# An adaLN block with attention and experts on one core: softmax inverses spread by DMA, copies and splits moved between engines

## The reference

```python
h = layernorm(x) * (1 + ca) + sa                    # x: 8 x 512 x 128
q, k, v = h @ Wq.T, h @ Wk.T, h @ Wv.T              # 16 heads of 64
q, k = l2norm(q) * q_scale, l2norm(k) * k_scale
attn = softmax(q @ k.T * 64 ** -0.5)                # 16 x 512 x 512 in each batch
x = x + ga * ((attn @ v) @ Wo.T + bo)
h = layernorm(x) * (1 + cb) + sb
x = x + gb * (moe(h))                               # top 2 of 8 experts with capacities, plus a shared expert
```

## Time and profile before

| | |
|---|---|
| median of 3 runs | 1409.95 us (1408.2 to 1410.84) |
| profiled execution | 1406.78 us, of which the span of the core is 1405.0 us |
| busy share of the span | TensorE 90%, VectorE 79%, ScalarE 68%, GpSimd 61% |
| mean granted TensorE clock | 0.959 of full speed |

### The profile page before, as it was taken

How to read it: one execution, slowest core, us unless ns; L and a number is a source line. 1 busy time by engine, 2 the same in 40 slices (tenths; PEclk the granted TensorE clock), 3 DMA queues, 4 the chain that set the end, 5 groups by cost and what they waited for, 6 DMA issues and landing times. The chain is left out here.

```text
span 1405.0 us, 31811 instructions
## 1 busy us (share of the span) xinstructions
PE 1262.1 (90%) x9674; PEld 828.6 (59%) x9674; DVE 1107.3 (79%) x1995; ACT 952.9 (68%) x2014; POOL 858.0 (61%) x1659
## 2 busy tenths in 40 slices
PE   4899999989999999999899999999994477899997
PEld 4555565656555565556566555666552355677775
DVE  3778878878878887788788788877873996788887
ACT  3677677767666776677677766777762565777776
POOL 2577666766666776666667667676754664444443
PEclk8899999999999999999999999999998699999999
DMA  5000000000000000000000000000002000535341
GB/s 131 2 2 1 2 1 2 2 4 2 1 4 2 2 2 4 2 2 2 4 1 2 3 2 2 2 1 2 2 1 75 1 0 9 131 86 104 89 89 38
DMA packets 53202, 28.60 MB, mean 20 GB/s; under 512 B 8720, under 2 KB 51224, under 8 KB 53016
## 3 DMA queue, kind: packets, MB, share of 16 engines
q1 hardware_dynamic: 51832, 25.99, 7.7%
q10 hardware_dynamic: 1184, 0.40, 0.1%
HBM read 24.16 MB, written 2.23 MB: 19 GB/s over the span
## 5 line engine op out<-in xcount | busy, mean ns | idle before, releaser
L697 ACT ACTIVATE probs<-bank,neg_max 128x512 f32<-128x512 f32 x512 | 347.5, 684 | 280.3 <-DVE neg_max L815 259.5
L815 DVE TENSOR_REDUCE neg_max<-bank 128x1 f32<-128x512 f32 x512 | 329.3, 685 | 165.4 <-PE bank L516 162.0
L556 PE MATMUL bank<-probsT,qkv 128*64 128x512 f32 x1024 | 280.7, 628 | 0.9 <-DVE oT L832 0.9
L516 PE MATMUL bank<-operands 64*128 64x512 f32 x1536 | 255.9, 439 | 0.9 <-DVE operands L810 0.5
L993 POOL TENSOR_TENSOR inv_wide<-inv_sum,consts 128x512 f32<-128x512 f32 x64 | 66.5, 1039 | 237.7 <-DVE inv_sum L826 237.7
L532 PEld LDWEIGHTS T<-ident,probs 64*128 64x128 f32 x4096 | 173.6, 142 | 40.3 <-issue 10.2
L532 PE MATMUL T<-ident,probs 64*128 64x64 f32 x4096 | 173.6, 226 | 1.5 <-issue 0.7
L486 PEld LDWEIGHTS bank<-operands,hT_h 128*128 128x128 f32 x254 | 48.2, 190 | 213.0 <-issue 209.4
L516 PEld LDWEIGHTS bank<-operands 64*128 64x128 f32 x1536 | 128.4, 190 | 63.5 <-issue 44.2
L1627 POOL TENSOR_TENSOR hid_l<-gated,hid_h 128x512 fp32r<-128x512 f32 x64 | 89.4, 1397 | 123.3 <-ACT hid_h L1544 123.3
L977 POOL TENSOR_TENSOR sq<-qkv 128x256 f32<-128x256 f32 x252 | 150.9, 615 | 11.9 <-ACT qkv L676 9.7
(11 more groups left out here) (235 smaller groups left out, 2399.7 us busy)
## 6 DMA issues: line engine op xcount, KB each, us to landing
probsT<-gate_scratch SPq DMA_DIRECT2D x64, 256.0 KB, 4.9
out<-x_all SPq DMA_DIRECT2D x8, 256.0 KB, 2.3
probsT<-in_L_ffn_fc_w SPq DMA_DIRECT2D x1, 1024.0 KB, 9.4
raw<-in_L_attn_Wq SPq DMA_DIRECT2D x1, 512.0 KB, 4.4
raw<-in_L_attn_Wk SPq DMA_DIRECT2D x1, 512.0 KB, 7.3
raw<-in_L_attn_Wv SPq DMA_DIRECT2D x1, 512.0 KB, 8.6
raw_o<-in_L_attn_Wo SPq DMA_DIRECT2D x1, 512.0 KB, 8.7
probsT<-in_L_ffn_sh_w SPq DMA_DIRECT2D x2, 256.0 KB, 2.7
```

Of the source, the lines that this page charges most:

```text
L516: last = nc.tensor.matmul(s_bank(hp, 2 * pair + head)[:], own[rows, q, toks], own[rows, k], start=((q, k) == (QH, KH)), stop=(q == QL))
L556: last = nc.tensor.matmul(O_BANK[rows, :], qkv[:, hp % 4, j, cols], probsT[:, hp % 2, head, j], start=(j == 0), stop=(j == NT - 1), skip_g ...
L697: nc.scalar.activation(probs[:, i % 4], s_bank(hp, i)[:], ACT.Exp, bias=neg_max[:, i:i + 1], accum_out=row_sum[:, hp % 2, i:i + 1]).then_i ...
L815: nc.vector.reduce_max(neg_max[:, i:i + 1], s_bank(hp, i)[:], AX.X, negate=True).then_inc(max_done, 1)
```

## The change

Four things. VectorE's copy of pair 2 goes to ScalarE, so ScalarE copies pairs 1, 2 and 3 and VectorE pair 0; ScalarE does pair 2 in pair 0 of the next slot, behind that pair's two exponentials, and no longer copies inverses. The inverses don't go through GpSimd, TensorE and ScalarE: SyncE writes the 128 x 8 inverses of a unit to DRAM, waits until they are there, and reads them back with two DMAs, one for each head, each spread over 64 partitions; VectorE's `normalise` waits for both. `ln_rows` is written with `scalar_tensor_tensor`, whose second operand is the inverse deviation broadcast over the row, in place of `tensor_scalar` with two scalars per partition. And `split_h1` moves from VectorE to GpSimd, at the end of head pair 5, all four tiles in a row; the high part is a multiplication by one.

```diff
                 for t in range(NT):
-                    last = nc.vector.tensor_scalar(h_ln[:, t], tile_of(b, t), mean_var[:, t, 0:1], rstd[:, t:t + 1],
-                                                   ALU.subtract, ALU.mult)
+                    last = nc.vector.scalar_tensor_tensor(out=h_ln[:, t], in0=tile_of(b, t), scalar=mean_var[:, t, 0:1],
+                                                          in1=rstd[:, t:t + 1].to_broadcast([P, C]), op0=ALU.subtract,
+                                                          op1=ALU.mult)
...
                 def _(sp):
+                    def spread_inverse(w, hp):
+
+                        sp.wait_ge(inv_done, w + 1)
+                        sp.dma_start(inv_scratch[hp % 2].rearrange("k q -> q k"), inv_sum[:, hp % 2]).then_inc(inv_out, 16)
+                        sp.wait_ge(inv_out, 16 * (w + 1))
+                        for head in range(2):
+                            sp.dma_start(inv_row[head * DH:(head + 1) * DH, hp % 2].rearrange("p (t q) -> p t q", t=NT),
+                                         inv_scratch[hp % 2].rearrange("(t h) q -> h t q", h=2)[head].partition_broadcast(DH)
+                                         ).then_inc(inv_in, 16)
...
                     def transpose_probs(u, pair):
-                        before, count = ((t_act, 0), (t_dve, 1), (t_act, 1), (t_dve, 2))[pair]
-                        after(pe, before, 2 * u + count)
+                        before, value = ((t_act, 3 * u), (t_dve, u + 1), (t_act, 3 * u + 1), (t_act, 3 * u + 2))[pair]
+                        after(pe, before, value)
...
-                            if pair == 1 and earlier >= 1:
-                                inverse_rows(u - 1, side)
-                                side = (r_copied, u)
...
-                            if pair == 1 and earlier >= 1:
-                                copy_inverse(u - 1, hp - 1)
...
-                            if pair == 1 and earlier >= 1:
-                                copy_transposed(u - 1, hp - 1, 3)
+                            if pair < 2 and earlier >= 1:
+                                copy_transposed(u - 1, hp - 1, pair + 2)
...
                     def normalise(u, hp):
                         dve.wait_ge(av_step, NT * (u + 1))
-                        dve.wait_ge(r_copied, u + 1)
+                        dve.wait_ge(inv_in, 32 * (u + 1))
...
-                            if pair == 0 and earlier >= 1:
-                                copy_transposed(u - 1, hp - 1, 2)
...
-                        if earlier >= 1:
-                            widen(u - 1, hp - 1)
...
+                        nc.gpsimd.tensor_tensor(hT_h[:, toks], h1_out[:, toks], c1.to_broadcast([P, P]), ALU.mult).then_inc(h1h_done, 1)
+                        pool.wait_ge(h1h_done, NT * b + t + 1)
+                        nc.gpsimd.tensor_tensor(hT_l[:, toks], h1_out[:, toks], hT_h[:, toks].bitcast(F32),
+                                                ALU.subtract).then_inc(hT_ready, 1)
...
+                        if main and hp == HP - 3 and not is_const(b, LAST):
+                            for t in range(NT):
+                                split_h1(b + 1, t)
```

More of the change, by code:

```diff
@@ L400, in adaln_attention_moe @@
             inv_done = sem("inv_done")
-            wide_done = sem("wide_done")
-            r_ready = sem("r_ready")
-            r_copied = sem("r_copied")
+            inv_out = sem("inv_out")
+            inv_in = sem("inv_in")
             av_step = sem("av_step")
@@ L467, in _, with batch @@
                 def _(sp):
+                    def spread_inverse(w, hp):
[6 more added lines that the diff above has]
+                                         ).then_inc(inv_in, 16)
+                    def batch(b):
+                        for hp in range(HP):
+                            if not (is_const(b, 0) and hp == 0):
+                                spread_inverse(HP * b + hp - 1, hp - 1)
+                    over_batches(sp, batch)
+                    spread_inverse(HP * B - 1, HP - 1)
                     sp.wait_ge(av_step, NT * HP * B)
@@ L535, in transpose_probs @@
                         last.then_inc(t_ready, 1)
[L537 to L545, removed]
                     def weigh_values(u, hp, j):
                         if j == 0:
-                            pe.wait_ge(t_dve, 2 * (u + 1))
-                            pe.wait_ge(t_act, 2 * (u + 1))
+                            pe.wait_ge(t_dve, u + 1)
+                            pe.wait_ge(t_act, 3 * (u + 1))
                             after(pe, o_done, u)
@@ L824, in invert_sums @@
                         dve.wait_ge(p_done, S_TILES * (u + 1))
-                        after(dve, wide_done, u - 1)
+                        after(dve, inv_out, 16 * (u - 1))
                         nc.vector.reciprocal(inv_sum[:, hp % 2], row_sum[:, hp % 2]).then_inc(inv_done, 1)
@@ L838, in take_mod @@
                         last.then_inc(done, 1)
[L840 to L844, removed]
-                        dve.wait_ge(h1h_done, NT * b + t + 1)
-                        nc.vector.tensor_tensor(hT_l[:, toks], h1_out[:, toks], hT_h[:, toks].bitcast(F32),
-                                                ALU.subtract).then_inc(hT_ready, 1)
                     def add_y(b, k):
@@ L897, in norm_first @@
                             ln_rows(dve, *rows)
-                        if not is_const(b, LAST) and (hp, pair) in ((5, 1), (5, 2), (5, 3), (6, 0)):
-                            split_h1(b + 1, (pair - 1) % NT)
                     def norm_last(b, hp, pair):
@@ L927, in slot @@
                                 row_max(u, hp, 2 * pair)
+                                if pair == 0 and hp == YT_HP and not is_const(b, 0):
+                                    dve.wait_ge(x1_done, b)
                                 row_max(u, hp, 2 * pair + 1)
@@ L932, in slot @@
                                 low_k(u + 1, hp + 1)
-                            if main and pair == 0 and hp == YT_HP and not is_const(b, 0):
-                                dve.wait_ge(x1_done, b)
-                            if pair == 0 and earlier >= 1:
-                                copy_transposed(u - 1, hp - 1, 2)
                             if pair == 2 and main:
@@ L946, in _ @@
                     take_mod(mod1, (CA, SA), 0, mod1_done, (h1_done, 0))
-                    for t in range(NT):
-                        split_h1(0, t)
                     sum_squares(0)
@@ L987, in normalise_qk, with split_h1 @@
                             nc.gpsimd.tensor_tensor(rows, rows, by, ALU.mult).then_inc(qn_done, 1)
-                    def widen(u, hp):
-                        pool.wait_ge(inv_done, u + 1)
-                        after(pool, r_ready, u)
-                        src = inv_sum[:, hp % 2].rearrange("p (t h) -> p t h", h=2)
-                        nc.gpsimd.tensor_tensor(inv_wide[:], src.unsqueeze(3).to_broadcast([P, NT, 2, DH]),
-                                                c1.unsqueeze(2).unsqueeze(3).to_broadcast([P, NT, 2, DH]),
-                                                ALU.mult).then_inc(wide_done, 1)
+                    def split_h1(b, t):
+                        pool.wait_ge(h1_done, b + 1)
+                        after(pool, pj_ready, NT * (HP * b - 1) + t + 1)
+                        toks = slice(t * P, (t + 1) * P)
+                        nc.gpsimd.tensor_tensor(hT_h[:, toks], h1_out[:, toks], c1.to_broadcast([P, P]), ALU.mult).then_inc(h1h_done, 1)
+                        pool.wait_ge(h1h_done, NT * b + t + 1)
+                        nc.gpsimd.tensor_tensor(hT_l[:, toks], h1_out[:, toks], hT_h[:, toks].bitcast(F32),
+                                                ALU.subtract).then_inc(hT_ready, 1)
                     def split_o(u, hp):
@@ L1025, in batch @@
                             slot(b, hp)
+                    for t in range(NT):
+                        split_h1(0, t)
                     normalise_qk(0, 0)
```

8 lines of the change are left out of this document (2 added, 6 removed).

## The result

The changed kernel takes 1447.7 us (1445.2 to 1450.4), the one before on the same chip 1410.4. The ratio is 1.026, with a 95% interval of 1.023 to 1.029: slower by 37 us, where 15 us less were predicted, and outside the range.

A forecast was written before the change was run, and what follows sets the result against it. TensorE, busy for 90% of the span, was taken as nearly full. With the transposes' gain eaten by the copy's wait, 9 us net and 6 us from earlier scaled Q made 15 us less: 1395 us, range 1371 to 1415.

The forecast's parts named there:

- the DMAs: Per unit, one 4 KB write and two reads: chain some 10 us, needed some 20 us later, so no cost.
- the inverses: Transposes gone from TensorE in pair 1: 34 us if nothing replaced them; GpSimd's earlier scaled Q: 6 us.
- the copy: In pair 1, TensorE's transposes wait for ScalarE's copy of pair 2: 4.68 us a batch against 4.24 removed.
- VectorE's relief: VectorE loses a 1.22 us copy per slot, mostly hidden; earlier layer-norm rows win 0.5 and 0.4 us in head pairs 0 and 3.
- The rival that counted on the clock to stay up: Behind shorter layer-norm stands in head pairs 1 and 4, 15 places win 1.6 us each: 24 us more, 1371; chance 0.25.
- Rows and splits: Layer-norm rows stay 3.07 us; splits on GpSimd cost nothing, and 0.3 us is felt ahead of head pair 6's maxima.
- ScalarE as the bound: Rival: pair 1 rests on ScalarE's exponentials and copy; 0.5 us more per slot gives 1427; chance 0.18.
- The inverses come late: Rival: a DMA chain of over 20 us makes normalising wait in every slot; at 25 us, over 1500; chance 0.02.
- four signs named as wrong: Pair 1 3.0 us everywhere; clock up behind layer-norm rows; normalising waiting for a DMA; the copy's wait pushing pair 2.

The follow-up runs named there:

- run 8: Not a follow-up run: in "make the run 8 bytes or longer" it means a stretch of contiguous bytes in a DMA write, 8 bytes long.

## Why the prediction was wrong

**The step that failed is the DMAs.** The prediction sized the write by a load of 4 KB that landed after 4.7 us, looked only at who waits for the data, found 20 us of slack and wrote "Hidden, so nothing". The write took 9.6 us, and its chain with the reads (3.5 us) is inside the bounds of 5 to 15. In the loop the data was indeed in time. But the write has a second price that the step didn't ask for: what it does to engines that don't wait for it. While it is under way some of TensorE's semaphore updates come up to 3.7 us late, and ScalarE and VectorE stand for them. Of the 47.5 us between the profiled spans of the changed kernel and the one with 32-byte pieces, 39.9 lie in the slots: from the first slot's first projection of a token tile to the last one TensorE needs 1023.1 and 983.2 us. The rest is at the end, where the last unit has no slot to hide in. That was put at 1.2 us at most; with 32-byte pieces VectorE waits there 3.8 us for TensorE, as before, and in the changed kernel 11.3 for the DMA:

```profile
DVE oT L830 <- DMA inv_row<-inv_scratch: 11.3, 1, 11.3
```

**What was left is 7 us off, by two errors that cancel.** Without the 4-byte pieces the changed kernel takes 1402.1 where 1395 was predicted. By its parts the prediction had 34 + 6 = 40 us won by the inverses, 25 lost by the copy net of VectorE's relief (what remains between 40 and the sum of 15), 0 for the rest. Measured are 26, 11 and 7.

*The inverses.* Pair 1 became shorter by 0.44 us (3.56 to 3.12), not 0.53, in most slots, and by less in head pair 3 (3.38): 24.0 us over the slots of the profiled execution, not 34. GpSimd's scaled Q is early, as predicted: the 9.5 us of the earlier trace rows are 2.5. But pair 2, where Q is transposed, is shorter by 2.7 us in sum, not 6. Pair 0 of head pairs 1, 4 and 6 gave 7.3. Against these 34 us, about 9 went to something that wasn't in the sum, the edge of the loop (where the hardware loop goes from head pair 7 back to 0). In head pair 0 after it, the stage of pair 0 with the same operations (windows: length, busy us by engine, clock, DMA share, GB/s), in the kernel before and with the inverses in 32-byte pieces:

```profile
548.20:552.80 4.60, 4.60 (x35) 2.83 (x35) 3.96 (x9) 1.11 (x3) 2.27 (x7) 1.00 0.02 7
```
```profile
532.53:538.56 6.03, 6.03 (x36) 3.81 (x36) 3.94 (x9) 1.01 (x2) 3.24 (x13) 0.72 0.15 41
```
```profile
548.20 0.44 PE L486 MATMUL bank<-operands,hT_h 128*128 128x384 f32 x1 [1.86 <-issue]
```
```profile
532.53 0.44 PE L503 MATMUL bank<-operands,hT_h 128*128 128x384 f32 x1 [2.42 <-issue]
```

TensorE stands 1.86 us at the edge in the one and 2.42 in the other. Behind the first stand the granted clock is 1.00, behind the second it is 0.72 on average, so it was at the lower of its two levels (1.2 of 2.4 GHz) for part of the stage, and the matmuls of the output projection take 0.63 us in place of 0.39. This costs 1.3 us on average at each of five edges (5.79 to 6.03 us against 4.55 to 4.82), and the longer stand itself 0.5. The rival that counted on the clock to stay up had looked only at the stands behind the layer-norm rows.

*The copy.* The wait is there as worked out. Head pair 3, with the copy on ScalarE (inverses in 32-byte pieces):

```profile
465.18 0.20 ACT L701 ACTIVATION_READ_ACCUMULATOR probs<-bank,neg_max 128x1 f32 x1
465.27 1.02 ACT L706 ACTIVATE probsT<-T 128x1024 f32<-128x1024 f32 x1
466.44 0.71 PE L549 MATMUL T<-ident,probs 64*128 64x64 f32 x16 [0.70 <-ACT probsT L706]
```

Reading, 0.09 us, copy, 0.15 us, transposes: the handoff is that of the prediction. Pair 1 is 4.22 us long there (predicted 4.16), 3.87 in head pair 5 (3.86), 3.62 in 7 (3.57). Over a batch from 412 us the eight pairs 1 sum up to 29.96 us against 25.2 without the copy: 4.7 us more, where 4.68 were predicted. But over the loop only 1.0 us of a batch is left. The rest comes back where TensorE had stood anyway: at the edge of the loop (0.5 us before it; behind it 1.5, since the clock stays up), in pair 0 of head pairs 1 and 4 (0.4 and 0.6), and in pairs 2 and 3 of head pairs 0, 3 and 5 (0.14 to 0.43). The stage that was shown above at 6.03 us, now with the copy:

```profile
539.59:544.08 4.49, 4.49 (x35) 2.90 (x35) 3.85 (x9) 1.00 (x2) 2.08 (x10) 1.00 0.05 8
```

The prediction had said this of head pairs 0 and 3 ("what pair 1 of these two slots wins or loses vanishes in that stand") and not of the other six.

*Rows and splits.* Put at 0 (the splits at 0.3 us a batch won), measured 7. The rows alone cost 3.5. Part of it is the clock once more: in the kernel with the rows alone, pair 0 behind the edges takes 6.00, 4.82, 6.03, 5.10 and 4.51 us, in the kernel before 4.82, 4.82, 4.63, 4.55 and 4.63. What tips it there, with rows of the same length, stays open.

**The rivals.** The clock's came true in part, in the places that it named. In pair 0 of head pairs 1 and 4 the clock stayed up in 4 of 12 cases with the inverses alone and in 5 of 12 with the copy. Two such stages of the kernel with the copy, the second at the lower clock like those of before, and the transposes that end TensorE's stand in each:

```profile
475.29:480.84 5.55, 3.75 (x36) 2.26 (x34) 5.37 (x12) 3.95 (x8) 2.23 (x7) 1.00 0.01 1
347.35:354.45 7.10, 5.30 (x36) 2.91 (x34) 5.43 (x12) 5.06 (x12) 3.33 (x13) 0.76 0.01 2
```
```profile
477.88 0.63 PE L592 MATMUL bank<-ident,h_ln 128*128 128x128 f32 x4 [1.80 <-DVE operands L807]
349.95 0.63 PE L592 MATMUL bank<-ident,h_ln 128*128 128x128 f32 x4 [1.80 <-DVE operands L807]
```

The stands are equally long, 1.80 us, and the stage with the clock up is 1.55 us shorter, where 1.6 was priced. Which of the two a batch gets is not told apart by any run here. ScalarE as the bound had the right sign and the wrong place: the three parts without the DMA are level with before. "The inverses come late" was the DMA's only rival, and got 0.02; it isn't what happened either: the DMA was asked for its delay and not for its neighbours. TensorE's busy time fell by 12 us (1262.1 to 1250.3), not by 30. Of the four signs named as wrong, one came at full size, once (normalising waits for the DMA at the end), one in part (the clock), and neither is what made the kernel slow.

## What to carry to other kernels

Ask of a new DMA three things: when its data is needed, into how many pieces of which size it falls, and what its transfer does to engines that don't wait for it. A transposing store of single fp32 values is to be avoided even if nobody waits for it; make the run 8 bytes or longer, or turn the tile on TensorE first. A wait that ends with a transfer on which the waiting engine does not depend is the sign of it; before giving it a cause, look which semaphore ends it. And a stand that grows by half a microsecond can cost three times that if the clock falls behind it.

## What the runs showed of the hardware that was not expected

- A write of 1024 pieces of 4 bytes takes 9.6 us of SyncE's time, 512 pieces of 8 bytes 3.3, 128 pieces of 32 bytes 1.5; 1024 pieces of 8 bytes land after 5.1 us, of 32 bytes after 3.0.
- With the 4-byte pieces 126 of 1409 semaphore updates of TensorE come more than 0.5 us behind the end of their matmul, mostly about when the write lands, and ScalarE and VectorE stand for them for up to 4.2 us (5.5 in the kernel with the DMA alone); this costs 35 to 46 us of 1410, and 19 with half of the pieces. Without such pieces none is later than 0.05 us.
- 512 KB more for each unit in pieces of 512 bytes, which raise the share of the data queue from 12.4 to 20.8%, cost nothing.
- Behind a stand of 1.86 us (2.06 in the kernel with 32-byte pieces) TensorE's granted clock was 1.00; behind 2.42 and 2.70 us it was 0.72 over the next stage of 6 us. Behind two stands of 1.80 us it was 1.00 once and 0.76 once over the whole stage, so the length of the stand doesn't decide it alone.
